# Switch layer: one-matrix blocks of 128 slots with resident expert weights, in place of blocks of 256 slots with streamed weights

## What is computed

```python
def _L1_ffn_ref(x, Wr, br, W1, b1, W2, b2):
    xt = x.reshape(-1, Hd)
    probs = jax.nn.softmax(xt @ Wr + br, axis=-1)
    gate = jnp.max(probs, axis=-1)
    idx = jnp.argmax(probs, axis=-1)
    h1 = jnp.maximum(jnp.einsum('th,ehf->etf', xt, W1) + b1[:, None, :], 0.0)
    ye = jnp.einsum('etf,efh->eth', h1, W2) + b2[:, None, :]
    onehot = jax.nn.one_hot(idx, n_exp, dtype=xt.dtype)
    y = jnp.einsum('te,eth->th', onehot, ye) * gate[:, None]
    return y.reshape(B, S, Hd)
```

## Time and profile before

| what | value |
| --- | --- |
| median of three runs | 3238.1 us (3233.96 to 3245.65) |
| the profiled execution's own time | 3249.25 us |
| its span, first to last instruction | 3247.5 us |
| mean granted TensorE clock | 0.933 |
| loop of the switch layer, first fetch to last send | 778.46 to 910.49 us |
| answers read back and added | 911.84 to 923.19 us |
| busy over the span | PE 88%, DVE 51%, ACT 46%, POOL 43% |

### The profile page before, as it was taken

The page is one execution under the profiler, slowest core; times in us unless marked ns, Lnnn a source line. Parts: engine busy times, 40 slices in busy tenths (PEclk is TensorE's granted clock), DMA queues, the critical chain, the costliest instruction groups (busy, mean ns, idle before and its releaser), DMA issues. The chain is left out here.

```text
span 3247.5 us, 45058 instructions
## 1 busy us (share of the span) xinstructions
PE 2851.5 (88%) x14331; PEld 1790.2 (55%) x14358; DVE 1642.2 (51%) x3968; ACT 1508.1 (46%) x3014; POOL 1403.3 (43%) x1281
## 2 busy tenths in 40 slices
PE   6886995986759989757979999999999998999998
PEld 4566995775623333337963444444444444677776
DVE  4445444553139999974234555555555555211111
ACT  3431332321348777622325665666665664344443
POOL 0012774523739999933324555555555554000000
PEclk9896997876969999988988999999999999899999
DMA  5002664002622222220030000000000000000000
GB/s 167 0 26 75 207 201 123 1 15 81 168 72 74 80 76 76 78 85 24 25 123 1 1 0 0 0 0 0 0 1 0 0 1 1 13 13 6 13 6 26
DMA packets 96120, 151.21 MB, mean 47 GB/s; under 512 B 13203, under 2 KB 48934, under 8 KB 95958
## 3 DMA queue, kind: packets, MB, share of 16 engines
q1 hardware_dynamic: 85334, 127.88, 12.6%
q0 software_dynamic: 10240, 20.99, 2.9%
q10 hardware_dynamic: 384, 0.46, 0.1%
HBM read 132.18 MB, written 25.50 MB: 49 GB/s over the span
## 5 line engine op out<-in xcount | busy, mean ns | idle before, releaser
L1456 POOL TENSOR_TENSOR l3a_p<-l3a_p,l3a_rden 128x512 f32<-128x512 f32 x512 | 521.5, 1040 | 487.0 <-DVE l3a_rden L1495 484.3
L1485 DVE CUSTOM_DVE_ANT_0 l3a_p<-bank,l3a_bias 128x512 f32<-128x512 f32 x512 | 333.4, 689 | 199.4 <-PE bank L1634 192.5
L1555 ACT ACTIVATE l3a_p<-l3a_p,l3a_low 128x512 f32<-128x512 f32 x512 | 365.4, 718 | 7.5 <-DVE l3a_low L1485 7.5
L1643 PEld LDWEIGHTS bank<-ident,l3a_p 128*128 128x128 f32 x2048 | 228.3, 140 | 167.2 <-issue 158.0
L2351 POOL TENSOR_TENSOR l2a_dBu<-l2a_du,l2a_bs 128x1024 f32<-128x1024 f32 x128 | 299.2, 2351 | 33.7 <-DVE l2a_h L2575 32.6
L1561 ACT COPY l3a_pT<-bank 128x512 f32<-128x512 f32 x256 | 150.4, 587 | 324.7 <-PE bank L1643 324.4
L2575 DVE TENSOR_TENSOR_SCAN l2a_h<-bank,l2a_dBu 128x1024 f32<-128x1024 f32 x128 | 290.4, 2280 | 8.7 <-ACT bank L2482 8.7
L1634 PE MATMUL bank<-l3a_kT,l3a_qT 64*128 64x512 f32 x1024 | 291.4, 645 | 1.0 <-ACT l3a_kT L1546 0.7
L1643 PE MATMUL bank<-ident,l3a_p 128*128 128x128 f32 x2048 | 274.9, 277 | 3.8 <-DVE l3a_pT L1491 3.2
L860 DVE SCALAR_TENSOR_TENSOR x<-bank,l3f_gates,x 128x128 f32 x256 | 85.5, 351 | 370.8 <-PE bank L888 370.8
L888 PEld LDWEIGHTS bank<-l3fe_w,l3fe_h 128*128 128x128 f32 x2048 | 233.7, 192 | 15.3 <-issue 15.3
(11 more groups left out here) (490 smaller groups left out, 4781.7 us busy)
## 6 DMA issues: line engine op xcount, KB each, us to landing
l2a_bs<-l2a_b_rows SPq DMA_DIRECT2D x128, 256.0 KB, 3.1
l0fe_wi<-in_L_ffn_in_dram SPq DMA_DIRECT2D x40, 516.0 KB, 4.8
l0fe_wo<-in_L_ffn_out_dram SPq DMA_DIRECT2D x40, 320.0 KB, 3.3
by_place<-by_distance SPq DMA_DIRECT2D x16, 512.0 KB, 14.3
l1fe_wo<-in_L_ffn_out_dram SPq DMA_DIRECT2D x24, 320.0 KB, 3.4
l3a_bias<-by_place SPq DMA_DIRECT2D x16, 448.0 KB, 13.1
l1fe_wi<-in_L_ffn_in_dram SPq DMA_DIRECT2D x24, 258.0 KB, 3.7
l0fe_answers<-l0f_y_rows SPq DMA_DIRECT2D x16, 256.0 KB, 4.9
```

The source lines that it names most:

```text
L1456: ins = pool.tensor_tensor(a, a, rden[:, t, h:h + 1].to_broadcast([P, S]), ALU.mult)
L1485: bk.drain(dve.tensor_tensor_reduce(p[u % 2][h][:, t, :], ps(job)[:], bias[:, u % HP * 2 + h, b0:b0 + S], 1.0, 3.0e38, ALU.add, ALU.min, l ...
L1555: ins = act.activation(a, a, ACT.Exp, bias=low[h][:, t:t + 1], scale=-1.0, accum_out=den[:, t, h:h + 1])
L1643: ins = pe.transpose(ps(job)[:, t * P:(t + 1) * P], p[u % 2][h][:, t, kt * P:(kt + 1) * P], chip.ident[:])
```

## The change

`GB` stays 256 for the first mixture layer. The switch layer gets a loop of its own, `switch_blocks`, with blocks of 128 slots: `blocks_of(1, 128)` = 40 blocks, 5120 slots. `place` takes the size as an argument.

- **Weights.** `SwitchWeights` allocates room for all eight experts' matrices for the time from the start of the program to the end of the switch layer. SP starts two DMAs for them (128x8x516 and 128x8x640) at the start of the feature attention, which had no program for SP before. In the loop ACT copies the block's `in` matrices (128x516) and DVE the `out` matrices (128x640) out of these into the rings `wi` and `wo`, each after a `value_load` of the expert number on its own sequencer. SP has nothing to do in the loop but the answers at its end.
- **POOL.** One fetch and one send for a block, 40 of each. NX = 8, NY = 4.
- **PE.** One transpose, four hidden products with N = 128, four answer products for a block; the order is turn_rows(b + 1), hidden(b), answer(b - 1).
- **ACT.** Four activations of 128x128 for a block, then the copy for block b + 2.
- **DVE.** take_rows(b + 1), take_answer(b - 1), then the copy for block b + 2, each for 128 columns but the copy of 640.

```diff
@@ place
-    NB = blocks_of(top)
-    MOST = NT * P // GB
-    NS = NB * GB // P
+    NB = blocks_of(top, size)
+    MOST = NT * P // size
+    NS = NB * size // P
@@ new
+class SwitchWeights:
+    NIN, NOUT = F + J, J * D + D
...
+    def load(self, sp):
+        sp.dma_start(self.all_in[:], self.w_in.rearrange("e p f -> p e f")).then_inc(self.loaded, 16)
+        sp.dma_start(self.all_out[:], self.w_out.rearrange("e p f -> p e f")).then_inc(self.loaded, 16)
@@ switch_blocks, POOL
+                def fetch(b):
+                    if b >= NX:
+                        pool.wait_ge(xT_turned, b - NX + 1)
+                        chip.apart(pool)
+                    pool.indirect_dma_start(xs[b % NX][:], None, xn_rows, ...)
+                def send(b):
+                    pool.wait_ge(y_ready, b + 1)
+                    chip.apart(pool)
+                    pool.indirect_dma_start(y_rows, ..., y[b % NY][:], None, ...)
+                for b in range(NX):
+                    fetch(b)
+                for b in range(NB):
+                    send(b)
+                    if b + NX < NB:
+                        fetch(b + NX)
@@ switch_blocks, ACT
+                def take_weights(b):
+                    e = act.value_load(expert[0:1, b:b + 1], min_val=0, max_val=E8 - 1)
+                    if b >= NW:
+                        act.wait_ge(h_ready, b - NW + 1)
+                        chip.apart(act)
+                    act.copy(wi[b % NW][:], held.all_in[:, bass.ds(e, 1), :].rearrange("p e f -> p (e f)")).then_inc(weights_in, 1)
...
+                for b in range(NB):
+                    act.wait_ge(weights_in, b + 1)
+                    act.wait_ge(h_summed, b + 1)
+                    if b >= 2:
+                        act.wait_ge(y_summed, b - 1)
+                    for j in range(J):
+                        ins = act.activation(h[b % 2][:, j, :], h_bank[b % 2][:, j * P:(j + 1) * P], act_fn,
+                                             bias=wi[b % NW][:, F + j:F + j + 1])
+                    ins.then_inc(h_ready, 1)
+                    if b + 2 < NB:
+                        take_weights(b + 2)
@@ switch_blocks, DVE
+                    dve.tensor_copy(wo[b % NW][:], held.all_out[:, bass.ds(e, 1), :].rearrange("p e f -> p (e f)")).then_inc(weights_out, 1)
...
+                for b in range(NB):
+                    if b + 1 < NB:
+                        take_rows(b + 1)
+                    if b:
+                        take_answer(b - 1)
+                    if b + 2 < NB:
+                        take_weights(b + 2)
@@ switch_blocks, PE
+                turn_rows(0)
+                for b in range(NB):
+                    if b + 1 < NB:
+                        turn_rows(b + 1)
+                    hidden(b)
+                    if b:
+                        answer(b - 1)
+                answer(NB - 1)
@@ feature_attention
+            @block.sync
+            def _(sp):
+                experts.load(sp)
```

More of the change, by code:

```diff
@@ L893, with blocks_of, place @@
 GB = 2 * P
-def blocks_of(top):
-    return ((top * NT * P + E8 * (GB - 1)) // GB + 1) // 2 * 2
-def place(chip, ctx, L, top, picks):
+def blocks_of(top, size):
+    return ((top * NT * P + E8 * (size - 1)) // size + 1) // 2 * 2
+def place(chip, ctx, L, top, picks, size):
     nc = chip.nc
-    NB = blocks_of(top)
-    MOST = NT * P // GB
-    NS = NB * GB // P
+    NB = blocks_of(top, size)
+    MOST = NT * P // size
+    NS = NB * size // P
     NK = top * NT
@@ L1010, in block_experts @@
     Q = GB // P
-    NB = blocks_of(top)
+    NB = blocks_of(top, GB)
     NIN, NOUT = w_in.shape[2], w_out.shape[2]
@@ L1186, in _, with top2_glu_experts @@
                 answer(NB - 1)
-def grouped_experts(chip, L, top, w_router, bias, w_in, w_out, act_fn, glu):
+def top2_glu_experts(chip, w):
+    L = "l0f"
     with ExitStack() as ctx:
         xn_rows = chip.nc.dram_tensor(f"{L}_xn_rows", (1 + NT * P, D), F32, kind="Internal").ap()
-        y_rows = chip.nc.dram_tensor(f"{L}_y_rows", (1 + top * NT * P + blocks_of(top) * GB, D), F32, kind="Internal").ap()
+        y_rows = chip.nc.dram_tensor(f"{L}_y_rows", (1 + 2 * NT * P + blocks_of(2, GB) * GB, D), F32, kind="Internal").ap()
@@ L1195, in grouped_experts @@
         with ExitStack() as first:
[L1196 to L1203, removed]
@@ L1206, in switch_experts, with __init__ @@
-def switch_experts(chip, w):
-    grouped_experts(chip, "l1f", 1, w["Wr"], w["br"], w["in"], w["out"], ACT.Relu, False)
+            normalise_and_route(chip, first, L, w["router_w"], turned_out=False, rows_out=xn_rows)
+        _, picks, pick_gates = route(chip, ctx, L, E8, None, top=2)
+        expert, source, target = place(chip, ctx, L, 2, picks, GB)
+        block_experts(chip, L, 2, xn_rows, y_rows, expert, source, target, pick_gates, w["in"], w["out"], ACT.Gelu_apprx_tanh, True)
+class SwitchWeights:
+    NIN, NOUT = F + J, J * D + D
+    def __init__(self, chip, ctx, w_in, w_out):
+        self.w_in, self.w_out = w_in, w_out
+        self.all_in, self.all_out = chip.sb(ctx, "switch_in", [P, E8, self.NIN]), chip.sb(ctx, "switch_out", [P, E8, self.NOUT])
+        self.loaded = chip.nc.alloc_semaphore(name="switch_loaded")
+    def load(self, sp):
+        sp.dma_start(self.all_in[:], self.w_in.rearrange("e p f -> p e f")).then_inc(self.loaded, 16)
+        sp.dma_start(self.all_out[:], self.w_out.rearrange("e p f -> p e f")).then_inc(self.loaded, 16)
@@ new lines, in switch_experts @@
+def switch_experts(chip, w, held):
+    L = "l1f"
+    with ExitStack() as ctx:
+        xn_rows = chip.nc.dram_tensor(f"{L}_xn_rows", (1 + NT * P, D), F32, kind="Internal").ap()
+        y_rows = chip.nc.dram_tensor(f"{L}_y_rows", (1 + NT * P + blocks_of(1, P) * P, D), F32, kind="Internal").ap()
+        with ExitStack() as first:
+            normalise_and_route(chip, first, L, w["Wr"], turned_out=False, rows_out=xn_rows)
+        _, picks, pick_gates = route(chip, ctx, L, E8, w["br"], top=1)
+        expert, source, target = place(chip, ctx, L, 1, picks, P)
+        switch_blocks(chip, L, xn_rows, y_rows, expert, source, target, pick_gates[:, 0, :], held, ACT.Relu)
@@ L2761, in build @@
         held = ScanWeights(chip, early)
+        between = ctx.enter_context(ExitStack())
+        experts = SwitchWeights(chip, between, a["L1_ffn_in"], a["L1_ffn_out"])
         earlier = ctx.enter_context(ExitStack())
@@ L2768, in build @@
             elif layer is feature_attention:
-                layer(chip, features)
+                layer(chip, features, experts)
                 earlier.close()
+            elif layer is switch_experts:
+                layer(chip, part(prefix), experts)
+                between.close()
             elif layer is selective_scan:
```

95 lines of the change are left out of this document (92 added, 3 removed).

## The result

| | before | after |
|---|---|---|
| median, us (range) | 3238.5 (3234.0 to 3245.7), 4 runs | 3213.1 (3207.2 to 3218.9), 4 runs |
| profiled execution, its span, us | 3249.25, 3247.5 | 3207.2, 3205.4 |
| mean granted clock | 0.933 | 0.942 |
| switch layer's loop, first fetch to end of last send, us | 132.03 | 109.66 |

The ratio is 0.9919, 95% interval 0.9901 to 0.9936: 25.4 us faster. The forecast was 3216 with a range of 3208 to 3232.

The account below looks back on a forecast made before the run. POOL's count of indirect-DMA issues was taken as the bound: first send at 792.3, plus 86.4, 9.0 and 1.0, ends the loop at 888.7 instead of 910.49, 21.8 us less; median 3238.1 becomes 3216 us, range 3208 to 3232.

Parts of the forecast that it names:

- 32 pairs: POOL's steady loop: one send and one fetch, each with its wait ahead, 2.70 us a pair, 86.4 us in all.
- seven sends and the last: End of POOL's loop: seven sends with their gaps, 9.0 us, then the last send, 0.98 us.
- POOL's bill of issues: Switch layer's loop: POOL is full, and its count of issues, 80 instead of 96, sets the end.
- The first send: POOL's first send in the loop starts at 792.3 us instead of 798.34, with ends of 790 and 795.
- rival 4: Early landings and an earlier clock rise bring the first send to 789 or before: 3212 us and less; chance 0.04.
- rival 1: VectorE's copy holds POOL up 0.50 us a block, 20 us in all, leaving 1.8 us gain: 3236 us; chance 0.08.
- The rule that spoke against the change: Float32 SBUF copies on VectorE block GpSimd's DMA descriptors, so POOL's period would grow by at least the copy's length.
- My only row against the rule: A DVE 128x512 SBUF copy, 0.54 us, beside which POOL's indirect DMA took its usual 1.01 us.
- The other engines: PE (2.1 us), ACT (1.9 us) and DVE (at most 2.0 us) stay below 2.70 us for a block.
- rival 2: ACT becomes the bound with the lookup in line, 2.9 us a block, gain 5 us: about 3230 us; chance 0.11.
- rival 3: PE's clock falls in the loop; at clock 0.50 it ends 39 us later: 3277 us; chance 0.06.
- Edits at nothing: The two large loads in the feature attention cost nothing; `place` changes within 0.3 us, taken as nothing.

Follow-up runs that it names:

- experiment 1: Changed kernel with the odd blocks' gathers left out, 60 indirect DMAs instead of 80: 3195.4 us, ratio 0.9869 against the kernel before.
- experiment 4: Changed kernel with both copies on ScalarE (0.9942, 0.9937), VectorE's copy doubled (0.9943, 0.9950), or each fetch issued twice with zero to three VectorE copies per block (1.0068).
- experiment 2: Kernel before with only the two resident weight loads added in the feature attention, read by nobody: 3237.5 us, ratio 0.9998.

## Why the prediction was right

The terms of its sum, each beside what the trace of the changed kernel has:

| term | predicted, us | measured, us |
|---|---|---|
| first fetch to first send | 13.8 | 10.98 |
| 32 pairs | 86.4 (2.70 each) | 88.59 (2.77 each) |
| seven sends and the last | 10.0 | 10.09 |
| loop | 110.2 | 109.66 |
| gain in the loop | 21.8 | 22.4 |

1. **POOL's bill of issues sets the end.** Right: the gaps are 0.30 us throughout, and taking 20 issues away took 23 us (experiment 1).
2. **The first send** was mis-sized by 2.9 us. From the first fetch it was 2.8 us to the first transpose (4.6 expected), since the early fetches landed in 2.5 to 3.7 us where the earlier trace rows have 2.5 to 5.2, and 8.9 us to the answer's addition (12.5 expected). I had priced both hidden steps at the low clock, 1.9 us each, but the clock rose during the second (granted 0.50, the lower of its two levels, from 774 to 778 us, and 0.99, the full level, from 778 to 784):

```profile
774.96 1.91 PE L1350 MATMUL bank<-l1fe_xT,l1fe_wi 128*128 128x128 f32 x8
...
776.88 1.63 PE L1350 MATMUL bank<-l1fe_xT,l1fe_wi 128*128 128x128 f32 x8
778.34 1.06 PE L1359 MATMUL bank<-l1fe_wo,l1fe_h 128*128 128x128 f32 x8
```

   The addition ended at 779.8, when POOL was in its seventh fetch and had the eighth to go, so the first send waited for POOL alone. Counted from the first fetch of the kernel before, that is a first send at 789.4, where rival 4 had 789 or before.
3. **The pair** was mis-sized by 0.07 us, 2.2 us over 32. That is rival 1 at a small price: the clean pair is 2.68 us, and the 22 lengthened DMAs among the pairs do the rest. The two errors nearly cancel, and it is luck that the sum is better than its terms.
4. **The rule that spoke against the change.** The rows show a DMA of 1.00 us grown to 1.29 when it began while a float32 copy from SBUF to SBUF ran on VectorE, and copies of 0.49 us grown to as much as 0.73 when they began in the later part of a DMA. The Trainium skill, "SBUF — State Buffer", section "SBUF: two separate sides", has such copies lock GpSimd out of the shared port. The trace agrees that there is such a hold, and that it lasts to the copy's end (experiment 4). It disagrees on what it costs here: by the copy's whole length for each block it would have been 20 us in the loop, and it was about 3 (80 issues, mean 1069 ns beside the 1032 ns of the kernel with both copies on ScalarE, on another chip), because the DMA waits at two moments only, and for what is then left of the copy.

   My only row against the rule was misread. Its operation took 0.54 us for 512 columns, which is 1.05 ns a column and not "faster than one column in a nanosecond". The copies of the earlier trace rows have a slope of 0.54 ns a column, and the new copy took 0.494 us for 640. So the row was not of the kind of the new copy, and gave nothing against rival 1, whose chance of 0.08 leaned on it. Whether the slower rate is why that DMA kept its 1.01 us isn't shown. A hold for a part of the copy should have been priced as a case of its own.
5. **The other engines.** ACT's turn 1.90 us (1.9 taken), PE's 1.90 (2.1; 779.34 to 781.24 from one block's hidden step to the next), DVE's copy 0.494 (0.50), its addition 0.292 (0.29), ACT's copy 0.636 (0.64), its four activations 1.14 (1.22): all below 2.70. The lookup lies beside the activations, so rival 2 did not come. The clock was 0.98 from 784 to 878 us, so rival 3 didn't either; PE waited for fetched rows and kept its level.
6. **Edits at nothing.** The loads cost nothing that shows (experiment 2), and `place` 0.1 us: the first fetch comes 28.0 us after the placing begins, 27.9 before.
7. **The total.** The medians differ by 25.4 us, the loops by 22.4. The other 3 us lie within the spread of four runs on either side; no stage is shown to have given them.

## To carry over

Where an engine shows 74% busy with the same short gap ahead of every instruction, it is full, and its bill is the count of its instructions: multiply that count, not the bytes. Halving a block's size pays only if what is loaded for each block goes with it, and keeping weights resident pays only if the issues go with it; here each half alone gave 12 and 0 us, and both 25. Before a copy between buffers is put on VectorE beside a full POOL, find where in POOL's DMAs it will fall: one that begins inside the copy grew by what was left of the copy less about 0.1 us, one that had the copy begin at its middle by 0.08 to 0.14 us, and the others by nothing. And before a row is used as evidence for another operation, divide its time by its columns.

## What was not expected of the hardware

- The hold between VectorE's copy of 0.49 us and POOL's indirect DMA depends on when the copy comes. The DMA took 0.10 to 0.29 us more if the copy began 0.06 to 0.25 us ahead of it, less than 0.1 from 0.27 us on, and nothing from about 0.36. It took nothing more if the copy began up to 0.42 us into it, and 0.08 to 0.14 if 0.51 to 0.56 us into it. A copy that alone began 0.59 to 0.78 us into a DMA left the DMA as it was and grew itself (0.53 to 0.75 us), so that it ended 1.30 to 1.35 us after the DMA's start. Each waits for the other's end, but the DMA has only two short stretches in which this matters.
- The same kernel is 1.7 to 2.1% longer on two of the chips. PE's results are taken up late there (a transpose after up to 7.7 us, on the first chip after 0.31 to 0.46), and gaps of up to 6.2 us follow in PE's row, in two of the layers. The cause is open. The gain of this change, 25.4 us where POOL was the bound, was 19.8 and 14.7 us there.
